# First attention of a two-layer kernel as one stream, with stacked fp32r scores and its projections in slots

## Chip, cores and metric

The kernel runs on one core of a Trainium2 chip. The metric is the device time of one execution in microseconds. TensorE multiplies, VectorE and ScalarE move and transform, GpSimd (POOL) does the rest, and SyncE (SP) issues most DMA transfers.

## Reference

Two layers, each an attention times the silu of a mixture of experts, are added to the residual. Only the first attention changes. It takes 8 sequences of 256 tokens with 256 features and 32 heads of 8:

```python
xn = _layernorm(x)
q = heads(xn @ wq.T + bq); k = heads(xn @ wk.T + bk); v = heads(xn @ wv.T + bv)
scores = jnp.einsum('bhqd,bhkd->bhqk', q, k) / np.sqrt(HD)
attn = softmax(where(causal, scores, -inf))
s = (attn @ v).reshape(B, S, H) @ wo.T + bo
g = silu(ffn0(xn))          # 8 experts, 2 chosen for each token, and a shared one
x = x + s * g               # then the second layer
```

## Kernel before

All of it is one program with one instruction stream for each engine. Its stages are the first attention (to about 419 us), the first experts' blocks (`pe_blocks0`), the second attention (`pe_slots`, eight sequences) and the second experts' blocks. Each engine's order is written out by hand and semaphores connect them.

The first attention goes over four turns (`TURNS`) of 512 tokens, two sequences each. A turn has 32 slots (`SLOTS`), and a slot handles two heads of one sequence. In slot s TensorE makes the scores of s (`scores`: L624 for the later 128 queries against 256 keys, L626 for the first 128 queries against 128 keys, L630 adds the causal mask as a bf16 product), then transposes the exponentials of slot s - 2 (`turn`, L640), and in each second slot multiplies four heads' transposes by the values (`pv`, L659 and L662). VectorE takes the largest score of each row (L839, L841) and copies the transposes out of PSUM (`copy_probs`, L780). ScalarE makes the exponentials and their sums (L742, L744). Scores of slot s wait for the exponentials of slot s - 2, because they use the same PSUM banks. A transpose waits for the copy that frees its bank.

Heads are 8 wide and TensorE's tiles 32 rows, so a tile holds four heads. The queries `qT` hold four heads as they are, and the keys `kTm` hold four copies with all but one head masked to zero (`keys`, L772, 128x512 each). The product is fp32.

A turn begins with what the turn before prepared. Beside the first slots TensorE makes the values (`values`, L561), the transposed activations of the next turn (L246) and the router's logits (`logits`, L568). When the last product by values is done, the boundary follows: `turn_inverse` (L673), `pe_queries_keys` of the next turn (L550), `project` (L684) and on the other engines `normalise`, `keep_out`, `queries` (L710) and `keys`. The routing of the first experts (`route0`) is VectorE's work in turn 2, and GpSimd scatters the rows in turn 3. At the program's start SyncE issues the constants, the experts' weights in one transfer of 4.9 MB and 15 MB of zeros (L2132) in eight transfers.

Of the kernel before, what the change touches and what calls it, by code (L numbers as in the profile page):

```python
# [19 lines left out]
F32 = mybir.dt.float32  # L20
# [25 lines left out]
LAG = 2  # L46

# [56 lines left out]
def build(nc, A, out, phases=3):  # L104
    with ExitStack() as ctx:
# [63 lines left out]
        MASK = cols[:, 0:4]  # L169
        G_NORM = cols[:, 12:13]  # L170
        BQ, BK, BV, BO = (cols[:, 4 + 2 * i:6 + 2 * i] for i in range(4))
# [89 lines left out]
        kTm = carve("attention", HPQ, KC, CH)  # L261
        qT = carve("attention", KC, CH)
# [3 lines left out]
        inv_wide = carve("attention", 2, ST * NH0, HD0)  # L266
        nmax = carve("attention", RING, ST, 2)
        total = carve("attention", 2, ST, NH0)
        inv0 = carve("attention", 2, ST * NH0)
        BLOCKS_AT = SPLIT1 + 2 * 512 + 32  # L270
        assert BLOCKS_AT > 2 * KC * CH + HPQ * KC * CH
# [25 lines left out]
        q_done, k_done, v_done = count("q_done", KC), count("k_done", KC), count("v_done", 2)  # L297
        qT_ready, v_ready = count("qT_ready", KC), count("v_ready", 2 * HPQ)
        keys_ready = count("keys_ready", KC * HPQ)
# [215 lines left out]
        ZERO_PARTS = -(-NB0 // TILES) - (-NB1 // TILES)  # L515
# [10 lines left out]
        ln_stats, ln_mean, ln_rstd = (carve("stay", *n) for n in ((2, 6), (TILES, 2), (TILES, 2)))  # L526
# [7 lines left out]
        def pair_of(s):  # L534

            w = s % PAIRS
            return s // PAIRS, w // (PAIRS // 2), (w % (PAIRS // 2)) // 2, (2 * (w % 2), 2 * (w % 2) + 1)

        def head_of(n):
            bb, mt, j, rows = pair_of(n // 2)  # L540
            return mt * (NH0 // KC) + rows[n % 2] * HPQ + j

        def pe_queries_keys(pe, t, mt):

            xT = norm0.xT
            if mt == 0:
                pe.wait_ge(norm0.xT_ready.sem, norm0.xT_ready.at(t, KC))
            for which, bank, done in ((0, 2 + mt, q_done), (1, 4 + mt, k_done)):
# [3 lines left out]
                last.then_inc(done.sem, 1)  # L552

        def pe_attention0(pe, t):
            xT = norm0.xT
            rows7 = ps[:, 7, :]
# [8 lines left out]
            def logits(turn):  # L565
                for c in range(CT):
                    for kc in range(KC):
                        last = pe.matmul(rows7[:, c * E0:(c + 1) * E0], xT[:, kc, c * P:(c + 1) * P], router0[:, kc, :],  # L568
                                         start=kc == 0, stop=kc == KC - 1)
                last.then_inc(lg0_done.sem, 1)  # L570
# [7 lines left out]
            def beside(s):  # L578
                if s == 0:
                    if t:  # L580
                        pe.wait_ge(s0_ready.sem, s0_ready.at(t - 1, 1))
                    values(0)
                if s == 1:
                    if t:
                        pe.wait_ge(s0_ready.sem, s0_ready.at(t - 1, 2))
                    values(1)
                if s == 3:
                    pe.wait_ge(v_ready.sem, v_ready.at(t, 2 * HPQ))
                    if t == 0:
                        logits(0)  # L590
                if t == TURNS - 2 and s == 22:
                    pe.wait_ge(o_copied.sem, o_copied.at(t, 1))
                    route0.pe_rank(pe, 6)
                if t < TURNS - 1:
                    if s == 5:
                        if t == 0:
                            pe.wait_ge(lg0_copied.sem, lg0_copied.at(0, 1))
                        norm0.pe_turn(pe, t + 1, 0, [rows7, rows7])
                    if s == 7:
                        pe.wait_ge(norm0.xT_ready.sem, norm0.xT_ready.at(t + 1, 1))  # L600
                        norm0.pe_turn(pe, t + 1, 1, [rows7, rows7])
                    if s == 10:
                        pe.wait_ge(norm0.xT_ready.sem, norm0.xT_ready.at(t + 1, 2))
                        logits(t + 1)
                if t == 0 and s == 12:
                    pe.wait_ge(lg0_copied.sem, lg0_copied.at(1, 1))
                    bias_row()

            def scores(s):

                bb, mt, j, rows = pair_of(s)
                q0 = bb * SEQ
                if s == 0:
                    pe.wait_ge(qT_ready.sem, qT_ready.at(t, KC))
                    pe.wait_ge(keys_ready.sem, keys_ready.at(t, HPQ))
                if s == PAIRS // 2:
                    pe.wait_ge(keys_ready.sem, keys_ready.at(t, KC * HPQ))
                if s >= 2:
                    pe.wait_ge(exp_done.sem, exp_done.at(t, 2 * s - 2))
                heads = [(2 * (s % 2) + hh, qT[32 * r:32 * r + 32, mt, :], kTm[32 * r:32 * r + 32, j, mt, :])  # L620
                         for hh, r in enumerate(rows)]

                for bank, q, k in heads:
                    pe.matmul(ps[:, bank, 0:SEQ], q[:, q0 + P:q0 + SEQ], k[:, q0:q0 + SEQ], start=True, stop=True)  # L624
                for bank, q, k in heads:
                    pe.matmul(ps[:, bank, SEQ:BLK], q[:, q0:q0 + P], k[:, q0:q0 + P], start=False, stop=True,  # L626
# [6 lines left out]
            def turn(s, hh):  # L633
                pe.wait_ge(exp_done.sem, exp_done.at(t, 2 * s + hh + 1))
                if s == 0 and hh == 0:
                    pe.wait_ge(keys_ready.sem, keys_ready.at(t, KC * HPQ))
                if s:
                    pe.wait_ge(probT_ready.sem, probT_ready.at(t, 2 * s - 1 + hh))
                for k in range(3):
                    last = pe.transpose(ps[:, 4 + hh, k * P:(k + 1) * P], prob[:, s % RING, hh, k * P:(k + 1) * P],  # L640
# [3 lines left out]
            def pv(s):  # L644


                bb, mt, j, _ = pair_of(s)
                if s == 0:
                    pe.wait_ge(v_ready.sem, v_ready.at(t, 2 * HPQ))
                if s == PAIRS:  # L650
                    if t == 0:
                        pe.wait_ge(bias_ready0, 2)
                    if t < TURNS - 1:
                        pe.wait_ge(lg0_copied.sem, lg0_copied.at(t + 1, 1))
                at = mt * SEQ
                pe.wait_ge(probT_ready.sem, probT_ready.at(t, 2 * s + 4))
                four = [(32 * r, probT[:, (s + n) % RINGT, hh, :]) for n in range(2) for hh, r in enumerate(pair_of(s + n)[3])]
# [8 lines left out]
            def turn_inverse(bb):  # L666
                pe.wait_ge(wide_ready.sem, wide_ready.at(t, bb + 1))
                if bb == 0:
                    pe.wait_ge(exp_done.sem, exp_done.at(t, HEADS2))
                wide = inv_wide[:, bb, :, :].rearrange("p n e -> p (n e)")  # L670
                for mt in range(KC):
                    for c in range(ST):
                        last = pe.transpose(ps[:, bb, mt * SEQ + c * P:mt * SEQ + (c + 1) * P],  # L673
                                            wide[:, c * D + mt * P:c * D + (mt + 1) * P], ident[:, :])
                last.then_inc(inv_turned.sem, 1)

            def project(bb):
                pe.wait_ge(o_ready.sem, o_ready.at(t, bb + 1))
                if t == TURNS - 2 and bb == 0:
                    pe.wait_ge(route0.rank_read.sem, route0.rank_read.at(0, 1))  # L680
                for c in range(ST):
                    for kc in range(KC):
                        at = (ST * bb + c) * P
                        last = pe.matmul(ps[:, 6 + bb, c * D:(c + 1) * D], oT0[:, kc, at:at + P], w0(3, kc, 0, D),  # L684
                                         start=kc == 0, stop=kc == KC - 1)
                last.then_inc(s0_done.sem, 1)

            for s in range(SLOTS + LAG + 1):
                if s < SLOTS:
                    scores(s)  # L690
                    beside(s)
                for hh in range(2):
                    if LAG <= s < SLOTS + LAG:
                        turn(s - LAG, hh)
                if s > LAG and (s - LAG) % 2 == 0:
                    pv(s - LAG - 2)
# [5 lines left out]
            if t < TURNS - 1:  # L702
                pe_queries_keys(pe, t + 1, 1)
            project(0)
            project(1)

# [1781 lines left out]
```

## Time and profile before

| | |
|---|---|
| median of 3 timed runs | 1941.01 us (1939.71 to 1941.13) |
| profiled execution | 1924.45 us |
| its span, first to last instruction | 1922.6 us |
| mean granted TensorE clock | 0.983 |
| TensorE busy | 1815.3 us, 94% |
| VectorE busy | 1282.4 us, 67% |
| ScalarE busy | 906.2 us, 47% |
| first attention, first score to last projection | 27.11 to 419.0 us |

The page's shares are means over four stages. The timeline rows give a start, a duration and a count. The durations of matmuls overlap, so the pace is read from one start to the next. An fp32 product is two MATMUL instructions in the trace, and the lists of order below count it once.

### The profile page before, as it was taken

To read this page: it belongs to the slowest core of one execution; us is meant where nothing else is said; L and a number is where in the kernel's file an instruction comes from. 1 tells how busy PE (TensorE), PEld (TensorE's weight loads), DVE (VectorE), ACT (ScalarE), POOL (GpSimd) and SP (SyncE) were. 2 spreads that over 40 slices of the span, in tenths; PEclk is the share of its full clock that TensorE was granted. 3 is DMA by queue.
4 is the path that set the end of the run, shared out by engine and by line. 5 is a ranking of instruction groups with operands and counts; after the bars stand their busy time and mean duration, and the time that the engine had idled before them with its cause. 6 is when DMAs were issued, how large, how long until landed. Compare 5 with 4: busy or idle time off the path is not lost.

```text
span 1922.6 us, 34586 instructions
## 1 busy us (share of the span) xinstructions
PE 1815.3 (94%) x11822; PEld 1443.5 (75%) x11822; DVE 1282.4 (67%) x2811; ACT 906.2 (47%) x2978; POOL 832.7 (43%) x919
## 2 busy tenths in 40 slices
PE   6999999999987999999999999999999997999986
PEld 4767666767765887788888888888888886777754
DVE  5678787863457788888676766667667664444467
ACT  3657564753433444445454455544545543444422
POOL 2000000320056665565767767777676773000066
PEclk9899999999999999999999999999999998999999
DMA  9600000123342000000000000000000223333344
GB/s 345 231 1 2 1 1 1 59 90 112 90 158 94 1 1 12 1 6 1 15 20 14 19 16 14 19 14 11 25 11 22 77 78 136 106 108 107 105 132 123
DMA packets 75907, 114.29 MB, mean 59 GB/s; under 512 B 9505, under 2 KB 65953, under 8 KB 73089
## 3 DMA queue, kind: packets, MB, share of 16 engines
q1 hardware_dynamic: 66416, 86.38, 13.6%
q0 software_dynamic: 9216, 25.18, 4.0%
q8 instruction: 75, 1.23, 0.3%
q10 hardware_dynamic: 144, 1.05, 0.1%
q14 instruction: 56, 0.45, 0.1%
HBM read 64.86 MB, written 47.71 MB: 59 GB/s over the span
## 4 chain that ended last, share of the span: by engine, by line
PE 77%; DVE 10%; POOL 5%; issue 3%; ACT 3%; DMA 2%; POOLq 0%; DVEq 0%; SPq 0%; ACTq 0%
PE ps L1356 11%; PE ps L1371 9%; PE ps L1443 5%; PE ps L1889 5%; PE ps L1397 4%; PE ps L640 4%; PE ps L624 3%; PE ps L1385 3%; PE ps L1384 3%; PE ps L1383 3%; PE ps L902 2%; POOL work L2084 2%; PE ps L1378 2%; PE ps L1906 2%; PE ps L1908 2%
## 5 line engine op out<-in xcount | busy, mean ns | idle before, releaser
L1356 PE MATMUL ps<-work,weights 128*128 128x256 f32 x1024 | 248.3, 386 | 1.1 <-DVE work L1629 1.1
L1371 PE MATMUL ps<-split 128*128 128x512 f32 x768 | 227.8, 419 | 0.0
L1356 PEld LDWEIGHTS ps<-work,weights 128*128 128x128 f32 x1024 | 186.4, 191 | 22.1 <-DVE work L1629 1.3
L1771 POOL TENSOR_TENSOR work<-work,rope 128x512 f32<-128x512 f32 x128 | 164.5, 1286 | 53.1 <-ACT work L1544 53.0
L1777 POOL TENSOR_TENSOR work<-work 128x512 f32<-128x512 f32 x128 | 164.4, 1284 | 5.0
L502 POOL DMA_INDIRECT xg<-work x96 | 96.9, 1009 | 153.1 <-PE ps L630 140.2
L2084 POOL DMA_INDIRECT work<-yg,work x64 | 62.4, 975 | 227.1 <-DMA yg<-work 207.3
L742 ACT ACTIVATE work<-ps,work 128x128 f32<-128x128 f32 x256 | 95.4, 373 | 124.3 <-DVE work L841 117.4
L1371 PEld LDWEIGHTS ps<-split 128*128 128x128 f32 x768 | 130.9, 190 | 24.6
L780 DVE COPY work<-ps 128x384 f32<-128x384 f32 x256 | 130.0, 549 | 8.5 <-PE ps L640 8.4
L1443 PE MATMUL ps<-weights,work 128*128 128x256 f32 x512 | 124.0, 386 | 2.5 <-ACT work L1600 2.5
L640 PE MATMUL ps<-ident,work 128*128 128x128 f32 x768 | 116.5, 283 | 8.1 <-DVE work L780 8.0
L1651 DVE TENSOR_TENSOR work<-ps,keep_w 128x384 f32<-128x384 f32 x128 | 65.4, 553 | 87.1 <-PE ps L1379 86.8
L744 ACT ACTIVATE work<-ps,work 128x256 f32<-128x256 f32 x256 | 122.4, 478 | 0.0
L2021 DVE SCALAR_TENSOR_TENSOR work<-work,ps 128x176 f32<-128x176 f32 (+1 forms) x95 | 35.0, 369 | 121.5 <-ACT work L1972 121.5
L1585 ACT ACTIVATE work<-ps,work 128x128 f32<-128x128 f32 x256 | 90.6, 366 | 51.4 <-PE ps L1385 51.1
L1443 PEld LDWEIGHTS ps<-weights,work 128*128 128x128 f32 x512 | 99.4, 195 | 16.8 <-ACT work L1600 3.1
L1664 DVE RECIPROCAL work<-ps 128x256 f32<-128x256 f32 x64 | 111.9, 1748 | 0.0
L1550 ACT COPY work<-ps 128x256 f32<-128x256 f32 x128 | 47.1, 368 | 130.3 <-PE ps L1371 130.3
L1889 PE MATMUL ps<-weights,work 128*128 x316 | 106.8, 461 | 0.2 <-ACT work L1966 0.2
L1383 PE MATMUL ps<-work 128*128 128x64 f32 (+1 forms) x512 | 97.3, 272 | 9.1 <-DVE work L1651 9.1
L640 PEld LDWEIGHTS ps<-ident,work 128*128 128x128 f32 x768 | 88.1, 145 | 22.8 <-issue 11.5
(236 smaller groups left out, 4508.8 us busy)
## 6 DMA issues: line engine op xcount, KB each, us to landing
work<-xg SPq DMA_DIRECT2D x118, 128.0 KB, 2.2
yg<-work SPq DMA_DIRECT2D x118, 128.0 KB, 1.7
xg<-work SPq DMA_DIRECT2D x6, 2048.0 KB, 17.8
weights<-in_w SPq DMA_DIRECT2D x8, 1024.0 KB, 9.4
weights<-in_f SPq DMA_DIRECT2D x8, 1024.0 KB, 5.1
weights<-in_f SPq DMA_DIRECT2D x1, 4864.0 KB, 16.0
work<-xn SPq DMA_DIRECT2D x32, 128.0 KB, 2.2
weights<-in_wo SPq DMA_DIRECT2D x1, 2048.0 KB, 8.6
```

The source lines that it names most:

```text
L640: last = pe.transpose(ps[:, 4 + hh, k * P:(k + 1) * P], prob[:, s % RING, hh, k * P:(k + 1) * P], ident[:, :])
L744: act.activation(pr[:, P:BLK], sc[:, 0:SEQ], ACT.Exp, bias=nmax[:, s % RING, 1, hh:hh + 1], accum_out=total[:, bb, 1, h:h + 1]).then_inc(e ...
L780: dve.tensor_copy(probT[:, s % RINGT, hh, :], ps[:, 4 + hh, 0:BLK]).then_inc(probT_ready.sem, 1)
L1356: last = pe.matmul(ps[:, 2, which * SEQ:(which + 1) * SEQ], w1(h, (which * KC + kc) * P, P), xT[:, kc, :], start=kc == 0, stop=kc == KC - 1)
L1371: last = pe.matmul(ps[:, 3, :], x1_split[:, xp, kc, c * P:(c + 1) * P], w_vg[:, n % 2, wp, kc, :], start=i == 0, stop=i == KC * len(TERMS) ...
L1383: pe.matmul(outs[0], left[:, 0:P], rhs[0], start=True, stop=True)
L1443: last = pe.matmul(ps[:, 7, c * D:(c + 1) * D], ogT[:, hh, c * P:(c + 1) * P], weights[:, W1O + h * D:W1O + (h + 1) * D], start=h == 0 and ...
L1664: dve.reciprocal(enz[:, n % 2, :, :].rearrange("p c n -> p (c n)"), ps[:, 0, SEQ:2 * SEQ])\
L1771: pool.tensor_tensor(qk[:, h % 4, :, :], raw[:, h % 2, :, :], rope[:, 0, :].unsqueeze(1).broadcast_to([P, 2, SEQ]), ALU.mult).then_inc(rot ...
L1777: pool.tensor_tensor(qk[:, h % 4, :, :], qk[:, h % 4, :, :], rot_s[:, h % 2, :, :], ALU.add)\
L1889: last = pe.matmul(ps[:, 2 + b % 2, 0:GUW], xb4T[:, b % 2, kc * P:(kc + 1) * P], experts1[:, bass.ds(offset[b] + kc * GUW, GUW)], start=kc ...
L2084: pool.indirect_dma_start(out=yk4[:, c % 2, k, :], out_offset=None, in_=yg1[:, :], in_offset=bass.IndirectOffsetOnAxis(ap=route1.index[:, ...
```

## The change

The first attention is one loop over 128 slots (`ALL`), without boundaries. Everything beside the scores, transposes and products by values has a slot number: `lower_bank` and `upper_bank` hold it for TensorE, which names the PSUM bank that is free then.

The four masked copies of the keys go. The projection of queries or keys of half the heads (`heads`) is copied with its bias (`act_heads`), then split into an fp32r upper part and an fp32r rest (`split_heads`: VectorE for turn 0, GpSimd later). Both parts are written to DRAM (`write_halves`) so that a head's 32 rows hold upper and rest of queries against upper and rest of keys in all four pairings, and come back as stacks of four heads (`load_stack`, `RINGQ` = 5 stacks, one for two slots). Score products are fp32r on 32 rows.

VectorE's other work stands between the largest values of a slot and its copies. The order of the weights' rows changes with the heads. Zeros are issued in 15 pieces and the experts' weights in eight, between the stacks.

```diff
-                heads = [(2 * (s % 2) + hh, qT[32 * r:32 * r + 32, mt, :], kTm[32 * r:32 * r + 32, j, mt, :])
+                if g % 2 == 0:
+                    pe.wait_ge(stack_loaded[n % RINGQ], 16 * (n // RINGQ + 1))
+                heads = [(2 * (g % 2) + hh, stack[32 * r:32 * r + 32, n % RINGQ, 0, :], stack[32 * r:32 * r + 32, n % RINGQ, 1, :])
...
-            turn_inverse(0)
-            if t < TURNS - 1:
-                pe.wait_ge(probT_ready.sem, probT_ready.at(t, HEADS2))
-                pe_queries_keys(pe, t + 1, 0)
-            turn_inverse(1)
-            if t < TURNS - 1:
-                pe_queries_keys(pe, t + 1, 1)
-            project(0)
-            project(1)
...
+            def lower_bank(t, s):
...
+                if s == 21 and t < TURNS:
+                    turn_inverse(t, 0)
+                if s == 23 and t < TURNS:
+                    project(t, 0)
+                if t < TURNS - 1:
+                    if s == 25:
+                        pe.wait_ge(s0_ready.sem, s0_ready.at(t, 1))
+                        values(0)
+                    if s == 27:
+                        pe.wait_ge(v_ready.sem, v_ready.at(t + 1, HPQ))
+                        heads(t + 1, 2, 6)
+                    if s == 29:
+                        pe.wait_ge(full_ready.sem, full_ready.at(t + 1, 3))
+                        heads(t + 1, 3, 6)
...
+            for g in range(ALL + 9):
+                t, s = divmod(g, SLOTS)
+                if g < ALL:
+                    scores(g)
+                lower_bank(t, s)
+                upper_bank(t, s)
+                for hh in range(2):
+                    if LAG <= g < ALL + LAG:
+                        turn(g - LAG, hh)
+                if LAG < g <= ALL + LAG and (g - LAG) % 2 == 0:
+                    pv(g - LAG - 2)
...
+        def split_heads(eng, t, n):
+            index, ring = t * PROJ + n, n % 2
+            eng.wait_ge(full_ready.sem, full_ready.at(t, n + 1))
+            if index >= 2:
+                eng.wait_ge(halves_written[ring], 16 * 4 * (index // 2))
+            eng.tensor_copy(halves[:, ring, 0, :], full[:, ring, :]).then_inc(upper_ready.sem, 1)
+            eng.wait_ge(upper_ready.sem, upper_ready.at(t, n + 1))
+            eng.tensor_tensor(halves[:, ring, 1, :], full[:, ring, :], halves[:, ring, 0, :], ALU.subtract).then_inc(lower_ready.sem, 1)
...
+            def load_stack(n):
+                t, i = divmod(n, STACKS)
+                bb, mt, j = i // (KC * HPQ), i // HPQ % KC, i % HPQ
+                for w in range(2):
+                    sp.wait_ge(halves_written[w], 16 * 4 * (t * KC + mt + 1))
+                if n >= RINGQ:
+                    sp.wait_ge(scores_done.sem, scores_done.at(0, 4 * (n - RINGQ) + 4))
```

TensorE at the end of a turn, before. L640 are transposes of exponentials, L659 and L662 products by values, L673 turned inverses, L550 the next queries and keys, L684 the projected output, L624 the first scores of the next turn:

```order
L640 MATMUL ps<-ident,work 128x128 x6
L659 MATMUL ps<-work,weights 32x256 x4
L662 MATMUL ps<-work,weights 32x128 x4
L673 MATMUL ps<-ident,work 128x128 x4
L550 MATMUL ps<-work,weights 128x512 x4
L673 MATMUL ps<-ident,work 128x128 x4
L550 MATMUL ps<-work,weights 128x512 x4
L684 MATMUL ps<-weights,work 128x256 x8
L624 MATMUL ps<-work 128x256 x2
```

TensorE in slots 15 to 17 of turn 0, changed. L689, L691 and L695 are a slot's scores and masks, L573 the next queries or keys of half the heads, L705 transposes, L724 and L727 products by values:

```order
L689 MATMUL ps<-split 128x256 x2
L691 MATMUL ps<-split 128x128 x2
L695 MATMUL ps<-causal_b,ident_b 128x256 x2
L573 MATMUL ps<-work,weights 128x512 x2
L705 MATMUL ps<-ident,work 128x128 x6
L689 MATMUL ps<-split 128x256 x2
L691 MATMUL ps<-split 128x128 x2
L695 MATMUL ps<-causal_b,ident_b 128x256 x2
L705 MATMUL ps<-ident,work 128x128 x6
L724 MATMUL ps<-work,weights 32x256 x4
L727 MATMUL ps<-work,weights 32x128 x4
```

The projections that stood together behind a turn now stand one by one behind the scores of a slot.

VectorE early in turn 1, before, with L839 and L841 the largest values, L780 the copies and L226 the scaling of the next activations:

```order
L839 TENSOR_REDUCE work<-ps 128x2
L841 TENSOR_REDUCE work<-ps 128x2
L780 COPY work<-ps 128x384 x2
L226 TENSOR_SCALAR work<-x_res,work 128x256 x4
L839 TENSOR_REDUCE work<-ps 128x2
```

VectorE in the middle of a turn, changed, with L905 and L907 the largest values, L827 the copies, L831 and L833 the inverse sums and their spreading:

```order
L905 TENSOR_REDUCE work<-ps 128x2
L907 TENSOR_REDUCE work<-ps 128x2
L831 RECIPROCAL work<-work 128x64
L833 COPY work<-work 128x512
L827 COPY work<-ps 128x384 x2
```

Other work stood behind the copies and stands ahead of them now.

SyncE behind the residual's load, before, with L2124 and L2127 the shared and routed experts' weights and L2132 the zeros:

```order
L2112 DMA weights<-in_w 128x2048
L2124 DMA weights<-in_sh 128x2176
L2127 DMA weights<-in_f 128x9728
L2132 DMA xg<-work 128x16x256 x2
L2132 DMA xg<-work 128x7x256
L2132 DMA xg<-work 128x16x256 x4
L2132 DMA xg<-work 128x15x256
```

SyncE at the same place, changed, with L2194 the written halves, L2204 the stacks and L2214 the zeros:

```order
L2194 DMA heads_by_part<-split 16x8x512 x8
L2204 DMA split<-heads_by_part 128x2x256 x4
L2194 DMA heads_by_part<-split 16x8x512 x8
L2204 DMA split<-heads_by_part 128x2x256 x4
L2214 DMA xg<-work 128x8x256
L2204 DMA split<-heads_by_part 128x2x256
L2214 DMA xg<-work 128x8x256
```

The written halves and the first stacks now come where the experts' weights were, and the zeros alternate with stacks.

## Rows read from the trace of the kernel before

**Rows 1.** The page, busy us, share and instructions of each engine

```profile
PE 1815.3 (94%) x11822; PEld 1443.5 (75%) x11822; DVE 1282.4 (67%) x2811; ACT 906.2 (47%) x2978; POOL 832.7 (43%) x919
```

**Rows 2.** Windows of the four turns: busy us of each engine, granted clock, DMA share, GB/s

```profile
27.11:133.84 106.73, 104.42 (x869) 75.21 (x868) 74.99 (x157) 59.72 (x272) 1.22 (x2) 0.89 0.51 180
133.84:229.40 95.56, 91.38 (x849) 65.66 (x848) 74.60 (x157) 59.69 (x271) 1.21 (x2) 1.00 0.01 2
229.40:333.00 103.60, 94.66 (x866) 66.99 (x865) 83.23 (x191) 59.88 (x272) 1.21 (x2) 0.98 0.01 1
333.00:419.00 86.00, 82.44 (x811) 60.23 (x811) 68.37 (x140) 57.24 (x266) 31.53 (x33) 1.00 0.16 57
```

**Rows 3.** Timeline of TensorE over a pair of slots: start us, us, group

```profile
200.74 0.64 PE L659 MATMUL ps<-work,weights 128*32 128x256 f32 x8
...
201.53 0.70 PE L624 MATMUL ps<-work 32*128 32x256 f32 x4
202.07 0.39 PE L626 MATMUL ps<-work 32*128 32x128 f32 x4
202.38 0.39 PE L630 MATMUL ps<-causal_b,ident_b 128*128 128x256 bf16 x2
202.61 0.82 PE L640 MATMUL ps<-ident,work 128*128 128x128 f32 x6
203.36 0.70 PE L624 MATMUL ps<-work 32*128 32x256 f32 x4
...
205.36 0.64 PE L659 MATMUL ps<-work,weights 128*32 128x256 f32 x8
```

**Rows 4.** Timeline of VectorE where it is behind

```profile
146.98 0.42 DVE L839 TENSOR_REDUCE work<-ps 128x2 f32<-128x256 f32 x1
147.31 0.68 DVE L841 TENSOR_REDUCE work<-ps 128x2 f32<-128x512 f32 x1
147.91 1.01 DVE L780 COPY work<-ps 128x384 f32<-128x384 f32 x2
148.84 0.42 DVE L839 TENSOR_REDUCE work<-ps 128x2 f32<-128x256 f32 x1
```

**Rows 5.** Timelines of TensorE and, last row, ScalarE behind turn 0

```profile
122.99 3.60 PE L550 MATMUL ps<-work,weights 128*128 128x512 f32 x8
...
130.30 3.62 PE L684 MATMUL ps<-weights,work 128*128 128x256 f32 x16
133.84 0.70 PE L624 MATMUL ps<-work 32*128 32x256 f32 x4
...
134.93 1.89 PE L561 MATMUL ps<-weights,work 128*128 128x256 f32 x8
...
138.48 0.37 ACT L742 ACTIVATE work<-ps,work 128x128 f32<-128x128 f32 x1 [9.01 <-DVE work L841]
```

**Rows 6.** Chain of work that ended last: start us, us, what

```profile
161.45 1.69 PE ps L568 x16
```

**Rows 7.** Timeline of TensorE, fp32r (L1340, L1343) and fp32 groups

```profile
896.98 0.48 PE L1340 MATMUL ps<-split,tri_r 128*128 128x256 f32 x2
897.29 0.34 PE L1343 MATMUL ps<-split,ones_r 128*128 128x128 f32 x2
897.47 1.95 PE L1356 MATMUL ps<-work,weights 128*128 128x256 f32 x8
```

**Rows 8.** Timeline of the start: first projections and their first copy

```profile
18.33 8.85 PE L550 MATMUL ps<-work,weights 128*128 128x512 f32 x16 [0.77 <-ACT work L255]
...
22.07 0.69 ACT L710 ACTIVATE work<-ps,bqs 128x512 f32<-128x512 f32 x1 [2.75 <-PE ps L550]
```

**Rows 9.** The page's costliest groups, GpSimd: busy us, mean ns of one

```profile
L1771 POOL TENSOR_TENSOR work<-work,rope 128x512 f32<-128x512 f32 x128 | 164.5, 1286 | 53.1 <-ACT work L1544 53.0
```

**Rows 10.** DMA issues of the execution: KB each, median us from issue to landing

```profile
xn<-work SPq DMA_DIRECT2D x8, 256.0 KB, 2.1
```

**Rows 11.** Windows in the slots of turn 0

```profile
64.00:72.00 8.00, 8.00 (x44) 5.88 (x34) 2.98 (x6) 2.68 (x14) 0.00 (x0) 0.50 1.01 338
...
100.00:110.00 10.00, 10.00 (x106) 7.08 (x108) 8.39 (x19) 7.65 (x38) 0.00 (x0) 1.00 0.01 2
```

More of the change, by code:

```diff
@@ L257, in build @@
         eps_row, eps_dk, zeros = minus_half[:, 16:32], minus_half[:, 32:32 + ST * 2], minus_half[:, 48:49]
-        kTm = carve("attention", HPQ, KC, CH)
-        qT = carve("attention", KC, CH)
+        stack = part(0, RINGQ, 2, SEQ)
+        halves = part(RINGQ * 2 * SEQ, 2, 2, CH)
+        FULL_AT = RINGQ * 2 * SEQ + 4 * CH
+        full = work[:, FULL_AT:FULL_AT + 2 * CH].rearrange("p (a n) -> p a n", a=2)
+        assert FULL_AT + 2 * CH <= SPLIT1
+        used["attention"] = SPLIT1
         oT0 = carve("attention", KC, CH)
@@ L576, in bias_row, with turn_inverse @@
                 last.then_inc(bias_done0, 1)
[L578 to L583, printed above, removed]
+            def turn_inverse(t, bb):
+                pe.wait_ge(wide_ready.sem, wide_ready.at(t, bb + 1))
+                pe.wait_ge(o_copied.sem, o_copied.at(t, bb + 1))
+                wide = inv_wide.rearrange("p n e -> p (n e)")
+                for mt in range(KC):
+                    for c in range(ST):
+                        last = pe.transpose(ps[:, 6 + bb, mt * SEQ + c * P:mt * SEQ + (c + 1) * P],
+                                            wide[:, c * D + mt * P:c * D + (mt + 1) * P], ident[:, :])
+                last.then_inc(inv_turned.sem, 1)
@@ new lines, in project @@
+            def project(t, bb):
+                pe.wait_ge(o_ready.sem, o_ready.at(t, bb + 1))
+                for c in range(ST):
+                    for kc in range(KC):
+                        at = (ST * bb + c) * P
+                        last = pe.matmul(ps[:, 6 + bb, c * D:(c + 1) * D], oT0[:, kc, at:at + P], w0(3, kc, 0, D),
+                                         start=kc == 0, stop=kc == KC - 1)
+                last.then_inc(s0_done.sem, 1)
+            def lower_bank(t, s):
+                if s == 1 and 0 < t < TURNS - 1:
+                    pe.wait_ge(full_ready.sem, full_ready.at(t, PROJ))
+                    logits(6)
+                if s == 1 and t == TURNS - 1:
+                    pe.wait_ge(full_ready.sem, full_ready.at(t, PROJ))
+                    pe.wait_ge(pow_rows, 7)
+                    route0.pe_rank(pe, 6)
+                if s == 21 and t < TURNS:
[12 more added lines that the diff above has]
+                        heads(t + 1, 3, 6)
@@ L601, in beside @@
                         norm0.pe_turn(pe, t + 1, 1, [rows7, rows7])
-                    if s == 10:
+                    if s == 15 and routed:
                         pe.wait_ge(norm0.xT_ready.sem, norm0.xT_ready.at(t + 1, 2))
[L604 to L619, printed above, removed]
-                heads = [(2 * (s % 2) + hh, qT[32 * r:32 * r + 32, mt, :], kTm[32 * r:32 * r + 32, j, mt, :])
+                        logits(7)
@@ L677, in project @@
[L677 to L686, printed above, removed]
@@ L862, in pe_blocks0 @@
+            for g in range(ALL + 9):
+                if g < ALL:
+                    largest(g)
+                beside(*divmod(g, SLOTS))
+                if LAG <= g < ALL + LAG:
+                    copy_probs(g - LAG)
         def pe_blocks0(pe):
@@ L2230, in _ @@
                 norm0.pool_all(pool, t)
+                for n in range(PROJ):
+                    split_heads(pool, t, n)
             pool.wait_ge(xg_zeroed, 16 * ZERO_PARTS)
@@ L2354, in _ @@
             act.copy(s2_split[:, :], weights[0:RS, W0S:W0S + NH1 * M]).then_inc(s2_upper, 1)
[L2355 to L2356 removed]
+            act_attention0(act)
             act_blocks0(act)
```

491 lines of the change are left out of this document (276 added, 215 removed).

## Prediction

> **What bounds the kernel now.** I began with the page's busy shares [rows 1]: TensorE is busy for 94% of the span and VectorE for 67%. The page shows no idle group of TensorE worth naming, so a gain has to come out of TensorE's own work or out of moments in which its work is thin. The diff touches the first stage alone, so I then cut that stage into its four turns [rows 2]: from the first score at 27.11 us to the end of the last projection at 419.0 us it takes 106.7 + 95.6 + 103.6 + 86.0 = 391.9 us. The second turn is the clean one (clock 1.00, no transfers, no routing). The first differs from it by 11.1 us, and its granted clock is 0.89. The third differs by 8.0 us, which is the routing on VectorE (83.2 us busy against 74.6).
>
> Third, the steady part of a turn [rows 3]. One pair of slots runs from 200.74 to 205.36 us, 4.62 us, or 2.31 us a slot, and the starts of the groups leave no hole on TensorE. In one slot the four 256-column score instructions take 0.54 us (201.53 to 202.07), the four 128-column ones 0.31, the two masks 0.23, the six transposes 0.75. The product by the values (L659, L662) adds 0.79 us to each second slot. VectorE keeps up with room to spare. Its own pace, where it is behind, stands in [rows 4]: from 146.98 to 148.84 us one slot takes it 1.86 us (largest values 0.33 + 0.60, two copies 0.93). ScalarE is busy for 59.7 of 95.6 us and sets nothing.
>
> Fourth, what a turn has beside its slots. At the boundary [rows 5] TensorE projects the next queries and keys (3.44 us for each half, 122.99 to 130.30 us with one group of four transposes between them), projects the output (3.54 us for 16 instructions) and makes the values (1.8 us for each half). Two transposed halves of the next activations and two turned inverses are four groups of four transposes, 0.5 us each at the pace of [rows 3], and the logits are 1.7 us [rows 6]. That makes 6.9 + 3.5 + 3.6 + 2.0 + 1.7 = 17.7 us. The clean turn is then 32 x 2.31 = 73.9, plus 17.7, plus 4.0 us of plain waits, in sum 95.6. Most of the 17.7 us lies at the boundary, where no scores flow: ScalarE stands for the last 9.0 us of it before its first exponential at 138.48 us [rows 5].
>
> **The change, part by part.**
>
> *Scores in fp32r.* An fp32 product is issued as two instructions, an fp32r product as one. The trace has no fp32r product on 32 rows, so I bound it. The nearest rows are L1340 and L1343 [rows 7]: two 256-column fp32r instructions take 0.31 us (896.98 to 897.29), two 128-column ones 0.18 us, on the whole array. Two heads in different row groups overlap today: four fp32 instructions in 0.54 us is 0.27 for two after another, and whole-array fp32 instructions follow each other in about 0.23 us (eight in 1.95, with the drain of the last). If fp32r pairs overlap likewise, both heads cost 0.16-0.2 us at 256 columns and 0.16 at 128, where two weight loads follow each other; I take 0.34 for both forms instead of 0.85, so 0.51 us less in a slot. If they don't overlap, 0.31 + 0.22 = 0.53, so 0.32 less. The low end, that an fp32r instruction on 32 rows is no faster than the two it replaces, gives nothing. I choose the overlap, since [rows 3] shows it for the same tiles. [...] The whole-array rows give 0.155 against 0.46 us for a product of 256 columns, a factor of 3.0, and the sum goes by them.
>
> *A slot after it.* TensorE's part falls from 2.31 to 1.80 us. VectorE needs 1.86 us. So a plain slot is no longer TensorE's: I take 2.0 us, VectorE's 1.86 and 0.14 for the hand-overs (an estimate between 1.86 and 2.31), because the transposes wait for its copies. The Trainium skill ("TensorEngine Tiling (Array Packing)", PSUM Bottleneck) warns that emptying PSUM may bind once the array is faster. [Rows 4] already says so here.
>
> *One stream, with the other work in slots.* The same 17.7 us now lies in 13 slots of a turn (1, 5, 7, 9, 11, 13, 15, 17, 21, 23, 25, 27, 29), behind the scores, while VectorE and ScalarE work. A turn is 19 plain slots x 2.0 = 38.0, plus 13 x 1.80 = 23.4, plus 17.7, in sum 79.1 us against 95.6. The last turn has no next heads, values or logits: 26 x 2.0 + 6 x 1.8 + 8 = 71 us. The tail behind the last slot was 10.0 us (409.0 to 419.0) and holds one projection instead of two: 8 us.
>
> *VectorE.* The eight masked key copies of a turn go, of 0.7 us each (as many columns as L710 of [rows 8]), 5.6 us at the boundary, which is already gone in the sum above; so nothing more. Its other work stands ahead of the copies instead of behind them. That lengthens the wait of one slot's transposes and shortens the wait of the next product; no value. The routing I leave at its 8 us: it is cut finer, but VectorE is now the fuller engine.
>
> *Split and round trip.* From turn 1 on GpSimd casts and subtracts, eight instructions a turn; [rows 9] has 1.29 us for its 128x512, so 10 us in 79, on an idle engine and one turn ahead. Nothing. The heads are written to DRAM (1 MB for each projection) and come back as 64 stacks of 256 KB, one for two slots, up to five ahead: 4 x 4.0 = 16 us of slack against a landing of 2.1 us for 256 KB [rows 10]. Zeroing (15 MB) and the experts' weights (5 MB) no longer stand in one block but go between the stacks. In turn 0 that is 1 MB of zeros and 0.26 MB of stack in a pair of slots of 79/16 = 4.9 us; zeroing moved 338 GB/s [rows 11], so it takes 3.9 us. It fits.
>
> *The start.* Only this is plainly worse. The 16 instructions of [rows 8] begin at 18.33 us, and ScalarE can copy the first half at 22.07. The second projection is ready at about 23.6. Then ScalarE's copy (0.69), VectorE's cast and difference (1.2), four issues (1.7) and the landing of 2 MB at about the rate of [rows 11]: 30 us. The first stack lands at 33 us. First score 33 instead of 27.1: 6 us lost.
>
> *Clock.* I keep the first turn's 11 us.
>
> **Sum.** 33 + 3 x 79.1 + 71 + 8 (tail) + 8 (routing) + 11 (clock) = 368 us, against 419.0: 51 us less. The span goes from 1922.6 to about 1872. The profiled execution took 1924.45 us, 16.6 less than the median 1941.01 of the three timed runs. The difference carries over, so 1941 - 51 = 1890 us.
>
> **Rivals.**
> - *The fp32r pairs don't overlap.* A slot costs TensorE 1.99 instead of 1.80: 13 x 0.19 and 19 x 0.1 make 4.4 us a turn, about 16 us in all: 1906 us. For it: no row shows such a pair. Chance 0.15.
> - *It works better.* The clock stays up in turn 0 (11 us) and slots come near 1.94, which gives 4 us more: 1876 us. Chance 0.10.
> - *Stacks come late.* Were the queue at 180 GB/s with both kinds of rows, a pair of turn 0 would need 7.3 us, 2.4 too many for 15 pairs, less 20 us of slack: 15 us, so 1905. Against it is the 338 GB/s of zeroing. Chance 0.08.
> - *fp32r gives nothing on 32 rows.* A turn is 32 x 2.31 + 17.7 = 91.6, 12.5 more: about 50 us come back, 1940 us, no change. Chance 0.04.
> - *The clock falls for long, slower than before.* [Rows 11] shows 8 us at a granted clock of 0.50, the 1.2 GHz level, with TensorE busy all the time in the same loop: 5.5 matmuls in a us against 10.6 at 2.4 GHz. The change takes work from the array and gives it a wait of some 5 us before the first score. A plain slot on TensorE would be 3.6-3.8 us instead of 2.0. At 1.8 us each, 28 slots, about 105 us at the low level beyond today's, which cost the 11 us, eat the 51 us; half of the stage at it gives 1941 + 60. The Trainium skill ("TensorE: Matmul & The Clock Gate", What's actually happening) says that sustained activity releases the throttle. The 8 us row shows a full TensorE that was not released for that long. Against it: turns 1 and 3 hold 1.00 [rows 2]. Chance 0.06.
>
> **How the numbers follow.** The forecast as summed has 0.57; its own range is 1877 to 1903. The rivals of 1906, 1905 and 1876 have 0.33. The range 1872 to 1912 holds all of these and leaves out the last two and the tails. 0.2% (4 us) is about what a measurement of this kernel can tell from no change. Faster by more 0.92, within it 0.03, slower 0.05.
>
> **What would show each step.** In the changed kernel's trace: the first score near 33 us; two score groups of about 0.17 us each before the masks; first scores of the turns about 80 us apart, with no 9 us wait of ScalarE between them; VectorE at 85% or more within a turn, and TensorE waiting before transposes on its copies; no wait of TensorE on a stack after the first; the last projection at about 368 us and the stages behind it unchanged. Wrong would be a plain pair above 4.4 us, a wait on stacks in turn 0, or a granted clock under 0.9 in two or more turns.

## The result, and the profile after

The changed kernel takes 1908.86 us (median of 4 runs, 1905.55 to 1910.86) against 1941.07 of the kernel before on the same chip: ratio 0.9831, 95% interval 0.9811 to 0.9852, or 32 us less. Forecast were 51 less, with a range from 1872 to 1912. The table tells where the other 19 us are to be sought. It divides the profiled executions into stages, each beginning with TensorE's first product of it; the last three columns are later runs, told below, all three on one chip.

| us | before | changed | before again | changed again | changed, 128 waits |
|---|---|---|---|---|---|
| first attention ends at | 418.8 | 368.2 | 419.8 | 366.6 | 367.2 |
| first experts | 194.5 | 195.6 | 195.6 | 192.6 | 194.7 |
| second attention | 1013.0 | 1031.8 | 1013.1 | 1029.4 | 1013.0 |
| last stage | 296.3 | 313.4 | 296.5 | 295.7 | 296.8 |
| span | 1922.6 | 1909.0 | 1925.2 | 1884.6 | 1871.9 |

The first attention gives 51 us, as summed. The second attention, which the diff doesn't touch, loses 19 of them (16 in the second profile of the changed kernel). (The last stage's 17 us more stand in its first profile alone; they are taken up among the open ends.) The page, in the manner of [rows 1], and its line on the queue that brings instructions:

```profile
PE 1774.0 (93%) x11310; PEld 1403.9 (74%) x11310; DVE 1268.0 (66%) x2787; ACT 908.8 (48%) x2986; POOL 857.1 (45%) x943
...
q8 instruction: 107, 1.75, 0.4%
```

The same line of the kernel before, which executes more instructions:

```profile
q8 instruction: 75, 1.23, 0.3%
```

The four turns of the changed kernel, to be held against [rows 2] (windows: busy us of PE, PEld, DVE, ACT, POOL; clock, DMA share, GB/s):

```profile
36.30:115.20 78.90, 75.98 (x668) 54.25 (x669) 64.94 (x140) 59.29 (x269) 14.77 (x13) 0.93 0.88 288
115.20:194.40 79.20, 76.29 (x722) 53.41 (x722) 69.21 (x150) 60.38 (x273) 8.76 (x10) 1.00 0.53 170
194.40:277.70 83.30, 79.54 (x738) 55.74 (x738) 73.91 (x168) 60.78 (x275) 8.76 (x10) 0.98 0.50 163
277.70:368.20 90.50, 78.06 (x746) 53.83 (x746) 74.31 (x162) 58.94 (x271) 31.92 (x33) 0.94 0.32 100
```

The second turn, at a granted clock of 1.00, takes 79.2 us where it took 95.6. (In six later profiles of the same code it takes 80.5 to 81.8 us at 0.96 to 0.98; the kernel before has 100.1 us at 0.95 in its second profile.) The timeline of TensorE gives the first score, a plain pair of slots (as [rows 3]) and the end of the stage:

```profile
36.34 0.58 PE L689 MATMUL ps<-split 32*128 32x256 f32 x2 [6.70 <-DMA split<-heads_by_part]
...
347.52 0.38 PE L689 MATMUL ps<-split 32*128 32x256 f32 x2
347.75 0.22 PE L691 MATMUL ps<-split 32*128 32x128 f32 x2
347.90 0.39 PE L695 MATMUL ps<-causal_b,ident_b 128*128 128x256 bf16 x2
...
349.96 0.99 PE L705 MATMUL ps<-ident,work 128*128 128x128 f32 x6 [0.16 <-DVE work L827]
...
351.67 0.38 PE L689 MATMUL ps<-split 32*128 32x256 f32 x2
...
364.73 3.65 PE L612 MATMUL ps<-weights,work 128*128 128x256 f32 x8 [0.78 <-DVE work L839]
368.21 0.60 PE L938 MATMUL ps<-ident,work 128*128 128x128 f32 x4
```

Read from start to start, the two score groups take 0.23 + 0.15 us, and a pair of slots 4.15 us. The transposes wait for VectorE's copy. VectorE shortly before, as [rows 4]:

```profile
344.53 0.68 DVE L907 TENSOR_REDUCE work<-ps 128x2 f32<-128x512 f32 x1
345.13 1.01 DVE L827 COPY work<-ps 128x384 f32<-128x384 f32 x2
346.06 0.41 DVE L905 TENSOR_REDUCE work<-ps 128x2 f32<-128x256 f32 x1
346.39 0.68 DVE L907 TENSOR_REDUCE work<-ps 128x2 f32<-128x512 f32 x1
346.99 1.01 DVE L827 COPY work<-ps 128x384 f32<-128x384 f32 x2
348.33 0.42 DVE L905 TENSOR_REDUCE work<-ps 128x2 f32<-128x256 f32 x1 [0.33 <-PE ps L695]
```

One slot of a pair runs at VectorE's 1.86 us (344.53 to 346.39), the next has 0.33 us of waiting for scores.

Now the second attention. TensorE's loop (`Fori`) covers sequences 2 to 6. TensorE at the jump back to the loop's start, in the changed kernel:

```profile
978.64 0.39 PE L1447 MATMUL ps<-work 128*128 128x128 f32 x2
978.87 0.39 PE L1448 MATMUL ps<-work 128*128 128x128 f32 x2
982.25 2.72 PE L1460 MATMUL ps<-work 64*128 64x256 f32 x16 [3.00 <-issue]
984.90 0.69 PE L1397 MATMUL ps<-s_split 96*128 96x128 f32 x2
```

"Issue" means that nothing shown in the profile was waited for. The view of TensorE's waits (us in total, times, longest) has four of these during the loop, one for each jump, and none in the kernel before:

```profile
PE ps L1460 <- issue: 11.0, 4, 3.0
```

The view of the DMA queues over the four sequences behind a jump (978.3 to 1480.6 us) shows what is fetched there (packets, MB, share):

```profile
q8 instruction: 36, 0.59, 0.5%
```

That is nine packets of 16 KB for each sequence. In the kernel before, over its four (1027.6 to 1512.2 us), this queue moves nothing at all: the whole loop stays loaded. The windows of that place and of one sequence show the second half of the price:

```profile
982.30:986.00 3.70, 3.70 (x20) 3.20 (x21) 1.02 (x3) 0.00 (x0) 0.18 (x1) 0.54 0.02 4
986.00:990.00 4.00, 4.00 (x25) 3.62 (x25) 2.57 (x9) 2.56 (x5) 2.02 (x2) 1.00 0.00 0
...
978.30:1104.70 126.40, 123.14 (x787) 105.00 (x786) 84.43 (x178) 60.25 (x177) 85.69 (x94) 0.99 0.05 18
```

After having stood for 3 us the engine is granted 0.54, nearly the 1.2 GHz level, for 3.7 us, and only then 1.00 again. The clock falls like this behind three of the four jumps. L1460's sixteen instructions take 2.72 us. A sequence of the kernel before takes 121.2 us:

```profile
1148.80:1270.00 121.20, 120.96 (x787) 103.67 (x786) 83.60 (x178) 60.50 (x177) 84.64 (x93) 1.00 0.04 15
```

### The profile page after: what moved, and what is told of

Same layout as the page of the kernel before. It is cut to its first block, busy times and chain, and to the rows that moved or that the text cites. A ratio compares the mean times of both kernels' runs of the same rounds, so it can differ in the third digit from the quotient of the medians.

```text
span 1909.0 us, 34158 instructions
## 1 busy us (share of the span) xinstructions
PE 1774.0 (93%) x11310; PEld 1403.9 (74%) x11310; DVE 1268.0 (66%) x2787; ACT 908.8 (48%) x2986; POOL 857.1 (45%) x943
## 4 chain that ended last, share of the span: by engine, by line
PE 78%; DVE 10%; issue 5%; POOL 3%; ACT 2%; DMA 2%; another core or an unknown queue 0%; SPq 0%; DVEq 0%; ACTq 0%; POOLq 0%
PE ps L1419 12%; PE ps L1434 9%; PE ps L1506 5%; PE ps L1952 5%; PE ps L1460 5%; PE ps L705 4%; PE ps L1448 3%; PE ps L1447 3%; PE ps L1446 3%; PE ps L959 2%; PE ps L1441 2%; PE ps L1969 2%; PE ps L1971 2%; PE ps L724 2%; PE ps L1980 2%
## 5 line engine op out<-in xcount | busy, mean ns | idle before, releaser
L827 DVE COPY work<-ps 128x384 f32<-128x384 f32 x256 | 129.7, 547 | 19.8 <-PE ps L705 19.5
L705 PE MATMUL ps<-ident,work 128*128 128x128 f32 x768 | 115.0, 281 | 17.5 <-DVE work L827 15.6
L705 PEld LDWEIGHTS ps<-ident,work 128*128 128x128 f32 x768 | 88.0, 144 | 42.6 <-ACT work L812 19.7
L1460 PE MATMUL ps<-work 64*128 64x256 f32 (+1 forms) x1024 | 104.3, 345 | 13.7 <-issue 11.0
L1460 PEld LDWEIGHTS ps<-work 64*128 64x128 f32 x1024 | 85.5, 192 | 29.8 <-issue 14.3
```

The lines of the kernel that those rows point to most:

```text
L827: dve.tensor_copy(probT[:, g % RINGT, hh, :], ps[:, 4 + hh, 0:BLK]).then_inc(probT_ready.sem, 1)
L1460: last = pe.matmul(ps[:, 4 + hh, at], k[rows, half, keys], q[rows, half, queries], start=half == 0, stop=half == 1)
```

## Experiments

**Theory and rival.** Counted in the trace (all its instructions in order of time), the loop has 1636 TensorE instructions. Its first is number 12840 of TensorE's before and 11878 after, since 1024 score instructions went and 62 waiting ones came. If instructions are loaded in blocks of 256, what matters is the number modulo 256: 40 before, 102 after. From 102 the loop may touch one block more than stays loaded, so that each jump back finds its target gone. The rival is any other cause of the 32 packets more: traffic, the other engines' loops (which grew by 30 and 24 register instructions), or chance.

**Moving the loop without changing it.** Instructions that wait for a semaphore long since raised stand ahead of TensorE's first work (two such waits make one instruction):

```diff
+            pe.wait_ge(pow_rows, 5)
+            for _ in range(2 * N):
+                pe.wait_ge(pow_rows, 5)
             pe.wait_ge(first_loaded, 16 * len(first_loads))
             norm0.pe_all(pe, 0)
```

The changed kernel unedited:

> The changed kernel once more, nothing edited. Theory (places are fixed by the program): TensorE stands for about 3 us at L1460 at the start of iterations 2 to 5 of the loop over sequences 2 to 6, and the page lists 107 packets of instructions. Rival (chance of one execution): the four stalls, or the stalls of 3 to 6 us behind 1810 us, are absent or elsewhere. Time near 1908.

N = 194:

> 194 instructions that only wait for a semaphore long since raised stand ahead of TensorE's first work, where it is idle for 15.6 us. The changed kernel has 962 TensorE instructions fewer ahead of its loop than the one before, 1024 gone and 62 added; with 194 more the loop starts at the same offset within a block of 256 instructions (16 KB, the size of the instruction packets) as before. Theory (the loop's 1740 instructions, 6.8 blocks, touch one block more in the changed kernel and are fetched anew in every iteration): packets fall from 107 to about 75, the four stalls at L1460 go, second attention ends about 19 us earlier, time 1889 to 1893. Rival (the fetches have another cause, such as the longer loops of VectorE and ScalarE or the DMA traffic): 107 packets and 1908 stay.

The kernel before with N = 62:

> The kernel before with 62 such waiting instructions ahead of TensorE's first work, and nothing else. Theory (place of the loop in its block): packets rise from 75 to about 107, TensorE stands for about 3 us at its loop's start in iterations 2 to 5, and the time rises by 12 to 19 us to 1953 to 1960. Rival: 75 packets and 1941.

N = 128:

> The changed kernel with 128 such waiting instructions instead of 194, a control. By the theory the loop still touches the extra block: 107 packets or nearly, four stalls, time near 1908. If any padding helps (a rival: the start of the program is what matters), it would be near 1890 like the one with 194.

N = 32 and N = 64, later:

> 32 waiting instructions. In the traces the loop's first instruction is TensorE's number 12840 before (40 modulo 256), 11878 in the changed kernel (102), 12006 with 128 waits (230), 12072 with 194 (40); the loop has 1636 instructions, 6 x 256 + 100, so it touches 7 blocks of 256 from 157 of the 256 offsets and 8 from the other 99. Numbers 40 and 230 run well and 102 does not; a stretch of 99 bad ones that holds 102 but not 40 holds 134 as well. Theory: with 32 waits (134) the loop is fetched anew each time, about 107 packets, 125 to 126 us a sequence. Rival (another rule than blocks of 256): 75 packets.

> 64 waiting instructions, number 166. The blocks allow both here: it tells on which side of 166 the bad stretch of 99 ends. Packets are near 107 with 125 to 126 us a sequence, or near 72 with 121.

| kernel | loop's first, mod 256 | packets | us a sequence behind a jump, mean of four | ratio to before (95%) |
|---|---|---|---|---|
| before | 40 | 75 | 121.2 | 1 |
| before, 62 waits | 102 | 111 | 124.9 | 1.0090 (1.0071 to 1.0109) |
| changed, again | 102 | 107 | 125.2 | 0.9824 (0.9808 to 0.9841) |
| changed, 32 waits | 134 | 107 | 125.6 | 0.983, one run of 1892.53 us |
| changed, 64 waits | 166 | 107 | 130.2 | 0.995, one run of 1913.98 us |
| changed, 194 waits | 40 | 72 | 121.2 | 0.9769 (0.9753 to 0.9785) |
| changed, 128 waits | 230 | 72 | 121.2 | 0.9749 (0.9733 to 0.9765) |

These runs are from another chip than the first, on which the kernel before takes 1923 us instead of 1941; the times expected for it were 18 us too high for that, so the ratios are to be read. The unedited kernel shows the four waits at the same line again, so they are no chance. The 62 waits alone put them into the kernel before (11.3 us in all, and 36 packets more), and its second attention grows from 1013.1 to 1028.8 us. The changed kernel's loop at another place loses nothing, so traffic and the other engines' loops are out. I had expected the 128 waits to fail as well. That was a wrong count of mine, 1740 instructions (fp32 transposes taken for two each, where the trace has one), which left only 53 good offsets. With 1636 the loop touches 7 blocks from 157 offsets and 8 from 99, and all seven rows fit one stretch of 99 bad offsets. The 194 waits cost 6.6 us at the start (first product at 24.9 instead of 18.3 us), which is why they give less.

64 waits are worse than 32, which the theory had left open. TensorE's timeline there:

```profile
979.59 0.39 PE L1448 MATMUL ps<-work 128*128 128x128 f32 x2
983.01 1.43 PE L1460 MATMUL ps<-work 64*128 64x256 f32 x6 [3.03 <-issue]
985.73 2.07 PE L1460 MATMUL ps<-work 64*128 64x256 f32 x10 [1.29 <-issue]
```

It stands twice in each of these sequences, the second time 14 instructions later and for 1.3 to 2.2 us. The simplest reading is that the jump's target lies shortly ahead of a block's end there, and the next block isn't loaded either. That would put the blocks' border near number 180 and the bad offsets from about 81 to 179, where 102, 134 and 166 lie. No run has its loop near these ends, so they are inferred.

**Fetching or jumping.** TensorE's loop written out, without waits:

```diff
-            with pe.Fori(2, SEQ_END) as t:
+            for t in range(2, SEQ_END):
                 pe_slots(pe, t, "middle")
```

> The changed kernel without padding, but TensorE's loop over sequences 2 to 6 is written out, so its 1636 instructions stand there five times and nothing jumps back. Theory (the cost is the jump to instructions that are no longer loaded, not the fetching): packets of instructions rise by some 30 or stay near 107, yet no stall at L1460's line and about 121 us a sequence: ratio near 0.975, as with 128 waits. Rival (fetching itself slows TensorE down): 125 us a sequence, ratio near 0.983.

96 packets, ratio 0.9752 (0.9732 to 0.9773), no wait by issue in these sequences, and a clean one:

```profile
1089.00:1210.10 121.10, 120.86 (x785) 103.53 (x784) 83.52 (x178) 60.45 (x175) 85.61 (x94) 1.00 0.05 18
```

A straight run of instructions is fetched at no cost that can be seen; the jump to unloaded ones costs the time. The Trainium skill ("Runtime: NRT & Kernel Launch", Instruction fetch mechanics) has blocks of 256 instructions, 2048 for TensorE, and warns that a taken branch whose target is no longer there waits for its fetch. That wait is what the traces show, 2.6 to 3.2 us each. But the section also speaks of a window of two blocks for branches. By that, each placing of this loop of 6.4 blocks would have to wait, and the well placed ones have neither a wait nor a packet in the loop; the measurement decides. A loop that touches 7 blocks runs well and one that touches 8 doesn't, as if one of TensorE's eight held what is fetched ahead; that last step no run shows.

**The kernel before once more**, for the stages:

> The kernel before once more with a profile, for its stages on the same chip as the others: 75 packets, 121 us for each of the sequences in the loop, and the part behind 1626 us at 284 us as in its first profile if its timed runs (1923 against 1941 on different chips) differ by the chip.

It has 75 packets, its sequences take 121.2 us, and its stages stand in the first table. The last one takes 296.5 us, as in the first profile (296.3).

**Parts of the change.** All four keep the 128 waits. The end of the stage is read as in the first table, at the first product behind it. First the score products in fp32:

```diff
-                    pe.matmul(ps[:, bank, 0:SEQ], q[:, P:SEQ], k[:, 0:SEQ], start=True, stop=True)
+                    pe.matmul(ps[:, bank, 0:SEQ], q[:, P:SEQ].bitcast(F32), k[:, 0:SEQ].bitcast(F32), start=True, stop=True)
```

(and the same for the 128-column product).

> The changed kernel with the 128 waiting instructions, and its 512 score products read as fp32 instead of fp32r. Theory (the prediction's prices): a score slot costs TensorE 0.5 us more, so it is the bound again at 2.31 us a slot; a turn is 91.6 instead of 79.1 us, the stage ends about 50 us later, and the time stands at 0.997 to 1.005 of the kernel before. Rival (the stream itself, not the fp32r products, brings half or more of the 51 us): the stage ends 25 us later or less, ratio 0.988 or less.

The stage ends at 414.7 instead of 367.2 us, 47.5 us later; ratio 0.9989 (0.9973 to 1.0004). TensorE over a plain pair:

```profile
392.54 0.70 PE L689 MATMUL ps<-split 32*128 32x256 f32 x4
393.07 0.39 PE L691 MATMUL ps<-split 32*128 32x128 f32 x4
393.39 0.39 PE L695 MATMUL ps<-causal_b,ident_b 128*128 128x256 bf16 x2
...
397.16 0.70 PE L689 MATMUL ps<-split 32*128 32x256 f32 x4
```

The pair takes 4.62 us, exactly that of [rows 3]. The stream and the slots without fp32r are worth 3 to 5 us (414.7 against 417.3 to 419.8 in three profiles of the old stage). That is a net: the first score comes 8 to 9 us later (36.3 against 27.0 to 28.3), and the four turns together are 12 to 13 us shorter (378.4 against 390.3 to 391.7).

VectorE's order:

```diff
-                beside(*divmod(g, SLOTS))
                 if LAG <= g < ALL + LAG:
                     copy_probs(g - LAG)
+                beside(*divmod(g, SLOTS))
```

> The same, but VectorE's other work stands behind its two copies of a slot, as in the kernel before. The prediction gave this order no value: then 0 to 3 us. Rival (the transposed probabilities are waited for less if the copies go first): faster by 5 us or more. Second rival (largest values are late if the other work stands between copies and the next largest values): slower by 5 us or more.

The stage ends at 368.0 against 367.2, ratio 0.9715 (0.9695 to 0.9735). Within the stage two effects offset each other. The second turn, at a granted 1.00, takes 81.6 us against 79.2 with the other work first, and the last one 86.6 against 87.6 to 90.5, most likely since its routing no longer delays the copies. The ratio lies below that of 128 waits by 0.003. The profile is the slowest of the four runs (1875.62 us, the others 1869.98 to 1872.75), and the two kernels ran on different chips, so whether this order gives up to 6 us or nothing stays open.

TensorE lighter (without `scores`' two mask products, L695, so that the causal mask is left out):

> The same without the causal mask's two bf16 products in each slot of the first attention (the mask is left out of the computation), 0.23 us less of TensorE in each slot. Theory (VectorE sets the plain slots, TensorE only the 13 with work beside): 13 x 0.23 a turn, about 12 us less in the stage. Rival (TensorE sets all slots): 32 x 0.23 a turn, 29 us less.

VectorE heavier:

```diff
...
+                dve.tensor_reduce(spare[:, g, :], sc[:, :, SEQ:BLK], AX.X, ALU.max, negate=True)
                 dve.tensor_reduce(nmax[:, g % RING, 0, :], sc[:, :, SEQ:BLK], AX.X, ALU.max, negate=True)\
```

> The same with VectorE's shorter largest value of each slot computed once more into a spare tile, 0.33 us more of VectorE in each slot. Theory (VectorE sets the plain slots): 19 plain slots x 0.3 a turn, 20 to 30 us more in the stage. If VectorE sets every slot, 32 x 0.33 a turn: 42 us. Rival (TensorE or the round of waits between engines sets the slots, and VectorE's 13% of idle time takes it in): 0 to 8 us.

| us | 128 waits | 0.23 us a slot less on TensorE | 0.33 us a slot more on VectorE |
|---|---|---|---|
| stage ends at | 367.2 | 358.3 | 389.2 |
| turn 1 (granted clock) | 81.8 (0.96) | 78.2 (0.96) | 82.5 (1.00) |
| a plain pair of slots, late in the last turn | 4.14 | 3.85 | 4.47 |
| a pair with half a projection | 5.26 | 5.13 | 5.25 to 5.39 |
| ratio to before | 0.9749 | 0.9666 | 0.9845 |

The starts of the scores in a plain pair, first with TensorE lighter, then with VectorE heavier:

```profile
340.15 0.38 PE L689 MATMUL ps<-split 32*128 32x256 f32 x2
341.66 0.38 PE L689 MATMUL ps<-split 32*128 32x256 f32 x2 [0.26 <-ACT work L808]
344.00 0.39 PE L689 MATMUL ps<-split 32*128 32x256 f32 x2
...
367.66 0.39 PE L690 MATMUL ps<-split 32*128 32x256 f32 x2
369.49 0.38 PE L690 MATMUL ps<-split 32*128 32x256 f32 x2 [0.36 <-ACT work L813]
372.13 0.38 PE L690 MATMUL ps<-split 32*128 32x256 f32 x2
```

The totals fall where the theory put them: TensorE's 0.23 us gives 8.9 us (about 12 expected, 29 if TensorE set all slots), and VectorE's 0.33 us costs 22.0 (20 to 30 expected, 42 if VectorE set all). The pairs show that the theory behind them is too simple. In a plain pair VectorE's 0.66 us more cost 0.33, so it sets one of the two slots; TensorE's 0.46 us less give 0.29 there, though the theory gave them nothing. In a pair with half a projection TensorE's 0.46 us give only 0.13. With VectorE heavier, the second turn costs 3.3 us more than 79.2 at the same clock, about half of 19 x 0.33, and 16 of the 22 us fall in the last two turns, where the routing stands ahead of the copies. So neither engine sets a kind of slot by itself; the slots follow the round of waits from scores to largest values, exponentials, transposes and copies. Both edits also ran at a lower granted clock in some turns (0.91 to 0.93), which these sizes contain.

## Why the prediction was right, and where not

*The time: 1890 forecast, 1908.86 measured.* That is outside the forecast's own 1877 to 1903. It lies in the range up to 1912 only by the room left for two rivals, fp32r pairs that don't overlap and stacks that come late, and neither happened. So the range held by luck.

*The stage: 368 forecast, 368.2 measured*, but some terms offset each other, so that it came out this close is luck as well.
- Score groups: 0.34 us forecast for both forms, 0.38 measured, so 0.47 us less a slot instead of 0.51. That is a factor of 2.2, less than the 3.0 of the whole-array rows. The pairs do overlap, so the first rival is out.
- A plain slot: 2.0 forecast, 2.07 measured. The Trainium skill ("TensorEngine Tiling (Array Packing)", PSUM Bottleneck) warns of this bound. The trace agrees for one slot of each pair (1.86 us, VectorE's own pace); the other takes 2.28 us, in which VectorE waits for scores.
- A clean turn: 79.1 forecast, 79.2 measured, 80.5 to 81.8 in later profiles with a granted clock of 0.96 to 0.98. It is right as a sum and not slot by slot: the pairs with half a projection take 5.26 us, 0.26 less than 2.0 + 1.80 + 1.72, and those with an output projection 6.03, 0.46 more than 2.0 + 1.80 + 1.77.
- The first score: 33 forecast, 36.3 measured, with a wait of 6.7 us on the first stack.
- *Clock and routing: two mis-sized terms that offset each other.* I kept 11 us for the clock of turn 0. It takes 78.9 us at a granted 0.93, as long as turn 1 at 1.00, but it also holds less work than the 79.1 I gave it (some 50 matmuls fewer: one output projection, one turned inverse, two slots' transposes and two products by values, with the bias row on top; about 4.5 us by the prediction's prices, an estimate). So the low clock cost about 4 us and not 11. The 11 us were no fixed price of turn 0 in the kernel before either: in its three profiles turn 0 takes 106.7, 99.4 and 102.8 us at 0.89, 1.00 and 0.95, while all four turns take 390.3 to 391.7. Against this, the start took 3.3 us more than forecast and the last two turns 7.7 us more: the third 83.3, the last with its tail 90.5, where 8 us of routing were put down for both together. In the new order VectorE's other work stands ahead of its copies. In the last turn the transposes wait for it, first behind 3.3 us of routing (282.06 to 285.42), then behind the inverse sums (L831, L833) and what had piled up:

```profile
286.12 1.46 PE L705 MATMUL ps<-ident,work 128*128 128x128 f32 x6 [3.05 <-DVE work L827]
293.21 1.51 PE L705 MATMUL ps<-ident,work 128*128 128x128 f32 x6 [1.90 <-DVE work L827]
```

  Both groups then take 1.5 us where they take 0.8 to 1.0 at full clock; the granted clock of this turn is 0.94.
- Stacks: the only wait of TensorE on one is the first. GpSimd's share and the round trip through DRAM made TensorE wait nowhere else, as said. The clock did not fall for long: 0.93, 1.00, 0.98 and 0.94 in the four turns. VectorE is busy for 82, 87, 89 and 82% of them, where 85% or more was expected in each.

*The step that failed* is the last one of the sum, that the span follows from the stage: "the stages behind it unchanged". I had looked for what the change does to the work behind it, and not for what it does to the place of the code. The four sequences behind a jump take 502.3 us (978.3 to 1480.6) against 4 x 121.2, so 17.5 us more: 11.0 are the waits, and about 5 of the rest the half clock behind three of them (an estimate: 3.7 us at 0.54, three times). With the loop moved back, the change gives what was forecast: 1874.50 against 1923.13, 48.6 us less, and 0.9749 of 1941.01 is 1892 against 1890 forecast.

*What stays open.* The last stage took 313.4 us in the changed kernel's first profile and 295.7 to 296.8 in the others of the table. ScalarE stands there nine times, for 32.6 us in all, in waits that no other of these profiles has, such as:

```profile
1839.42 0.48 ACT L2047 COPY work<-ps 128x384 f32<-128x384 f32 x1 [4.31 <-remote]
1845.76 0.46 ACT L2035 ACTIVATE work<-ps 128x352 f32<-128x352 f32 x1 [5.86 <-remote]
```

Timed runs of the kernel before differ by as much between the two chips (1941 and 1923), so I take these 17 us for the first chip's, the same in both kernels. The ratios fit that, 0.9831 on one chip and 0.9824 on the other. No profile of the kernel before from a 1941 us execution is there to show it, and no run asked what ScalarE waits for. Nor was fp32r tried in the old order with boundaries, so how much of the 47.5 us it needs the stream for isn't known. And only this one loop was moved: that the border lies between 7 and 8 blocks rests on five offsets of it.

## What to carry over

When an edit removes or adds instructions ahead of a loop, count the loop's instructions and find its place in the blocks of 256: this loop of TensorE, once it touched 8 blocks instead of 7, cost 4 us for each jump back and 9 us in the worst place. Compare the number of instruction packets before and after, look for instruction packets within the loop, and look for waits by issue at the loop's first line; some idle waiting instructions ahead of the first work, or writing the loop out, mend it (0.9749 with 128 waits, 0.9752 with the loop written out, 0.9824 with neither). When one engine is relieved, price the slot by the next fullest engine: a relief of 0.47 us on TensorE gave 0.24 us a plain slot. And check what stands ahead of that engine's copies, since what was harmless there before is now waited for.

## What the runs showed of the hardware

- A jump back to instructions that are not loaded: TensorE stands for 2.6 to 3.2 us at each; with 64 waits it stands a second time, for 1.3 to 2.2 us, 14 instructions on. Behind three of the four jumps in the changed kernel the granted clock falls (0.54 over 3.7 us behind the first).
- A TensorE loop of 1636 instructions: no instruction packet moves during it in the kernel before, 36 packets of 16 KB in four sequences once it starts at 102 instead of 40 modulo 256.
- 96 packets of 16 KB fetched in a straight line, 24 more than with the loop well placed, cost nothing measurable (0.9752 against 0.9749).
- An fp32 product of 32 rows and 256 columns in a pair costs 0.27 us, an fp32r one 0.10 to 0.12; for 128 columns 0.16 and 0.08 to 0.09.
- 194 instructions that only wait for a raised semaphore delayed TensorE's first product by 6.6 us, 128 of them not at all (TensorE is idle for 15.6 us there).
